# Last stage of a routed network: one sorted buffer of 136 tiles for two of 144, two routing batches, and a small GpSimd write ahead of each indirect transfer

## What is computed

```python
x = x + _L1_ffn_ref(_layernorm(x, axis=-1), router_w, w1, w2, w3)
...
h1 = jnp.einsum('nc,ehc->neh', flat, w1)
h3 = jnp.einsum('nc,ehc->neh', flat, w3)
h = jax.nn.silu(h1) * h3
y = jnp.einsum('neh,ech->nec', h, w2)
out = jnp.einsum('ne,nec->nc', gates, y)
```

## Time and profile before

| what | us |
|---|---|
| median of 3 runs | 1226.98 (1225.48 to 1228.63) |
| the profiled execution, by the clock of the runs | 1228.42 |
| its span in the profile | 1226.7 |
| mean clock granted to TensorE, as a share of 2.4 GHz | 0.952 |
| last stage: from its first up matmul to the end of the span | 809.3 to 1226.7 |
| last product (L1945) of the last stage starts | 1200.5 |

### The profile page before, as it was taken

One profiled execution on the slowest core, in us unless ns is written; L12 is line 12 of the kernel. 1 busy time (PEld: TensorE's weight loads), 2 busy tenths in 40 slices (PEclk: granted clock), 3 DMA queues, 4 the chain that ended last, 5 costly groups with the idle time before them and its releaser, 6 DMA issues.

```text
span 1226.7 us, 17966 instructions
## 1 busy us (share of the span) xinstructions
PE 1048.8 (85%) x5576; PEld 737.6 (60%) x5577; DVE 587.0 (48%) x1719; ACT 524.9 (43%) x980; POOL 502.7 (41%) x799
## 2 busy tenths in 40 slices
PE   4779966889998899998998989987779988988991
PEld 2334322567666544644873455467779888888891
DVE  7855873211064265555746634353273333333454
ACT  5567844234232476653357645544222222222220
POOL 5922265630633320000310366525336666565651
PEclk9799988999999999999999989999799999999996
DMA  9930001232322100000000111163255757668766
GB/s 278 365 154 1 1 33 63 78 93 69 94 78 78 29 18 0 1 1 0 1 1 1 64 43 45 38 179 112 78 180 187 242 167 258 189 225 312 239 199 226
DMA packets 100884, 135.53 MB, mean 110 GB/s; under 512 B 12434, under 2 KB 69570, under 8 KB 99906
## 3 DMA queue, kind: packets, MB, share of 16 engines
q1 hardware_dynamic: 88002, 108.00, 27.6%
q0 software_dynamic: 12800, 26.50, 6.6%
HBM read 88.81 MB, written 45.65 MB: 110 GB/s over the span
## 4 chain that ended last, share of the span: by engine, by line
PE 63%; DVE 14%; issue 8%; another core or an unknown queue 7%; ACT 5%; POOL 2%; DMA 1%; DVEq 0%; ACTq 0%; POOLq 0%; SPq 0%
PE bank L1263 14%; PE bank L1289 12%; PE bank L1270 9%; PE bank L1299 7%; PE bank L1148 4%; PE bank L1028 4%; PE bank L1183 2%; DVE sb_R L1945 2%; PE bank L1211 2%; PE bank L1200 1%; PE bank L994 1%; PE bank L1172 1%; DVE sb_R L1430 1%; PE bank L1192 1%
## 5 line engine op out<-in xcount | busy, mean ns | idle before, releaser
L1263 PE MATMUL bank<-sb_R,sb_wih_sb 128*128 128x512 f32 (+2 forms) x504 | 202.9, 553 | 12.5 <-ACT sb_R L879 6.6
L1945 DVE TENSOR_TENSOR sb_R<-sb_R,bank 114x384 f32<-114x384 f32 x144 | 79.6, 553 | 230.8 <-PE bank L1299 138.2
L879 ACT ACTIVATE sb_R<-bank,sb_lb_sb 128x512 f32<-128x512 f32 (+2 forms) x252 | 151.0, 633 | 88.6 <-PE bank L1270 78.4
L650 POOL DMA_INDIRECT expert_out<-sb_R,sb_slot_row x144 | 140.8, 977 | 111.3 <-DVE sb_R L1903 36.3
L913 ACT ACTIVATE sb_R<-bank 114x384 f32<-114x384 f32 x144 | 69.4, 490 | 250.0 <-PE bank L1289 123.4
L1263 PEld LDWEIGHTS bank<-sb_R,sb_wih_sb 128*128 128x128 f32 x504 | 96.4, 193 | 111.7 <-issue 82.7
L1289 PE MATMUL bank<-sb_xt,sb_BIG 128*114 128x128 f32 x864 | 111.0, 280 | 19.6 <-DVE sb_R L1945 15.0
L1299 PE MATMUL bank<-sb_BIG,sb_R 114*128 x864 | 123.6, 279 | 2.1 <-issue 1.6
L1289 PEld LDWEIGHTS bank<-sb_xt,sb_BIG 128*114 128x114 f32 x864 | 102.2, 183 | 23.9 <-issue 23.0
L644 POOL DMA_INDIRECT sb_R<-sorted_out,sb_dest_i x64 | 60.8, 950 | 125.7 <-DMA sorted_out<-sb_R 44.0
L1299 PEld LDWEIGHTS bank<-sb_BIG,sb_R 114*128 114x128 f32 x864 | 110.0, 194 | 2.5 <-issue 2.3
(11 more groups left out here) (279 smaller groups left out, 1691.5 us busy)
## 6 DMA issues: line engine op xcount, KB each, us to landing
sb_BIG<-up_t SPq DMA_DIRECT2D x72, 342.0 KB
sb_wih_sb<-up_t SPq DMA_DIRECT2D x36, 342.0 KB
sb_whh_sb<-up_t SPq DMA_DIRECT2D x36, 342.0 KB
sb_XS<-expert_in SPq DMA_DIRECT2D x18, 528.0 KB
expert_in<-sb_R SPq DMA_DIRECT2D x18, 512.0 KB, 6.0
sb_R<-expert_out SPq DMA_DIRECT2D x7, 1024.0 KB, 6.7
sorted_in<-sb_R SPq DMA_DIRECT2D x9, 512.0 KB, 5.5
sb_XS<-sorted_in SPq DMA_DIRECT2D x18, 256.0 KB
```

What stands on the lines that cost most here:

```text
L650: pool.indirect_dma_start(out=expert_out, out_offset=bass.IndirectOffsetOnAxis(ap=slot_row[:, i:i + 1], axis=0), in_=yd[i // 8 % RING][:, ...
L879: act.activation(gb[s][k][:, 0:c], bank[4 * s + k][:, 0:c], funcs[k], bias=lb_sb[:, (p - 1) * GATES + k:(p - 1) * GATES + k + 1]).then_inc ...
L1263: mm = pe.matmul(bank[4 * s + k][:, 0:c].rearrange("p (w b) -> p w b", b=GH), wih_sb[:, p - 1, k * P:(k + 1) * P], xin, start=True, stop=( ...
L1945: dve.tensor_tensor(hm[j % 2][0:HC, :], sl[j % 2][0:HC, :], bank[3 + 2 * (j % 2)][0:HC, 0:KU * P], ALU.mult).then_inc(d2_m, 1)
```

## The change

- The last stage has one sorted buffer, `expert_in`, of 136 tiles: 128 closed ones (`CLOSED1`) and one open tile for each expert, at the end. The tokens are placed in three batches (`BATCHES`): the first half of 32 token tiles as before during the LSTM, then two batches of 16. A batch fills whole tiles in the closed part; what is left over goes to the open tile of the expert, and a later batch fills that first.
- The loop has 17 groups of 8 tiles. Groups 0 to 6 need the first batch alone, groups 7 to 9 the second batch, and from the open group (10th in order) on they need the third (`READY` = 7, 10; `GROUPS`).
- The loop's extra work is put at other tiles: transposes and sums of the second half at tiles 0, 1, 2, 4, 6, 7, 8, 10, statistics in two batches, scores at 12 to 15 and 22 to 26, and each of the two batches is routed in 15 steps, one per tile, from tile 16 and from tile 30. The steps have more operations than before (`OpenPlaces`: 73 and 66 waiting operations for 47), on half as many tokens each. Two of the eight normalisations move from ACT to DVE.
- POOL's order is now 24 rows home, with the statistics ahead of rows 2 and 7, 32 sorting transfers (not before tile 28), 5 rows home, 32 sorting transfers (not before tile 52), 107 rows home (from tile 72), at the same pace of eight per five tiles. There are 392 indirect transfers.
- `pause()` stands ahead of every indirect transfer of the kernel, in the first expert layer too: POOL writes 0 to one column (`pause_p`, 128 x 1) and waits for the semaphore of that write.
- The loads of the final results start at group 14 of 17 (`D3_LOAD`), and their sums are spread over tiles 120 to 134.

```diff
+    CLOSED1 = 2 * NTILE
+    NS = CLOSED1 + E
+    BATCHES = ((0, NH), (NH, NH + NH // 2), (NH + NH // 2, NTILE))
+    READY = ((2 * NH - E + 1) // 8, (3 * NH - 2 * (E - 1)) // 8)
+    GROUPS = list(range(READY[1])) + [CLOSED1 // 8] + list(range(READY[1], CLOSED1 // 8))
...
-        T_TILES, RANK_TILE = 18, 21
-        Y_FIRST, IN_TILE, Y_TILE = 22, 26, 66
...
-        ND2 = HALVES * NSLOT1 // 8
-        D3_LOAD = ND2 - 5
+        T_AT = {1: 1, 2: 2, 4: 3, 6: 4, 7: 5, 8: 6, 10: 7}
+        XN_ACT_AT = {9: 0, 11: 2, 17: 4, 19: 5, 21: 6, 23: 7}
+        XN_DVE_AT = {9: 1, 11: 3}
+        R_AT = {12: 0, 13: 1, 14: 2, 15: 3, 22: 4, 24: 5, 25: 6, 26: 7}
+        ROUTE_AT = {1: 16, 2: 30}
+        HOME_FIRST, LN_AT, IN_AT, HOME_MORE, HOME_REST = 24, (2, 7), (28, 52), 29, 72
...
+        ND2 = NS // 8
+        HALF_GROUPS = (READY[1] + 1, ND2)
+        D3_LOAD = ND2 - 3
+        D3_ADD = 8 * (ND2 - 2)
...
             for g in range(1, ND2):
-                if g + 1 < ND2 and g + 1 != D2H:
+                if g + 1 < ND2 and g + 1 not in READY:
                     d2_load(g + 1)
+                if g == READY[0]:
+                    sp.wait_ge(rd.tiles, 2)
+                elif g == READY[1]:
+                    sp.wait_ge(rd.tiles, 3)
                 d2_weights(g)
-                if g + 1 == D2H:
-                    sp.wait_ge(s_scat[1][1], 32 * NH)
+                if g + 1 in READY:
+                    sp.wait_ge(s_scat[1][1 + READY.index(g + 1)], 16 * NH)
                     d2_load(g + 1)
...
+            def pause():
+                step(pool.memset(pause_p[:, :], 0.0))
+
...
                     for k in range(K):
+                        pause()
                         pool.indirect_dma_start(
...
             def rows_home(i):
+                pause()
                 pool.wait_ge(d2_yo, i + 1)
                 pool.indirect_dma_start(
...
+            def rows_in(b):
+                pool.wait_ge(rd.dest, b + 1)
+                lo, hi = BATCHES[b]
+                for i in range(2 * (hi - lo)):
+                    t, k = lo + i // 2, i % 2
+                    pause()
+                    pool.wait_ge(d2_h, IN_AT[b - 1] + 5 * i // 8)
+                    pool.indirect_dma_start(
+                        out=expert_in, out_offset=bass.IndirectOffsetOnAxis(ap=dest_i[:, k, t:t + 1], axis=0),
+                        in_=XR[:, t - NH, :], in_offset=None).then_inc(s_scat[1][b], 16)
...
+            for i in range(HOME_FIRST):
+                if i in LN_AT:
+                    t_finish(1, LN_AT.index(i), NGH // 2)
                 rows_home(i)
...
+            rows_in(1)
+            for i in range(HOME_FIRST, HOME_MORE):
+                rows_home(i)
+            rows_in(2)
+            for i in range(HOME_MORE, 8 * ND2):
+                pool.wait_ge(d2_h, min(HOME_REST + 5 * (i - HOME_MORE) // 8, 8 * ND2))
                 rows_home(i)
```

More of the change, by code:

```diff
@@ L444, in _ @@
             sp.wait_ge(w_in, W_ALL)
-            for rows in [sorted_in] + expert_in:
+            for rows in (sorted_in, expert_in):
                 zv = rows.rearrange("(p n) d -> p (n d)", p=P)
@@ L487, in d2_load @@
             def d2_load(g):
[L488 removed]
+                u = g % 2
                 if g >= 2:
@@ L616, in scatter @@
                     pool.wait_ge(zeroed, ZEROS)
-                rows, src = (sorted_in, XN[:, half * NH:(half + 1) * NH, :]) if layer == 0 else (expert_in[half], XR)
+                rows, src = (sorted_in, XN[:, half * NH:(half + 1) * NH, :]) if layer == 0 else (expert_in, XR)
                 for t in range(half * NH, (half + 1) * NH):
@@ L1029, in hidden, with rank @@
                               start=True, stop=True).then_inc(r.h, 1)
[L1031 to L1036 removed]
+            def rank(layer, r, b):
+                m = flat(space[layer, b].mask)
+                n = m.shape[1]
+                pe.wait_ge(r.mask, b + 1)
+                pe.matmul(bank[1][:, 0:n], before[:, :], m, start=True, stop=True)
+                pe.matmul(bank[1][:, n:2 * n], ones[:, :], m, start=True, stop=True).then_inc(r.ranks, 1)
             def b1_transposes(b):
@@ L1880, in _ @@
                         in_d[0].chosen(1)
-                    if half > 0 and n in (8, 9):
-                        in_d[0].weights(n - 8)
+                    if half > 0 and n == 8:
+                        in_d[0].weights(0)
+                    if half > 0 and n == 9:
+                        in_d[0].weights(1)
+                        in_d[0].weights(2)
                     if half > 0 and n == 10:
-                        in_d[0].counts()
+                        for part in range(3):
+                            in_d[0].counts(part)
                     if half > 0 and n == 11:
@@ L1922, in d2_slots, with d3_add, d2_route @@
                     dve.tensor_tensor(slot_row[:, cols], slot_k[:, cols], pad_row[:, cols], ALU.max).then_inc(d2_meta, 1)
-            def d3_add(i):
+            def d3_add(i, k):
                 t0, n = D3_BLOCKS[i]
                 xv = X[:, t0:t0 + n, :]
-                dve.wait_ge(y_in[i], 16)
-                for k in range(2):
-                    if k > 0:
-                        dve.wait_ge(d3_x, 2 * i + 1)
-                    dve.tensor_tensor(xv, both[i][:, :, k, :], xv, ALU.add).then_inc(d3_x, 1)
+                if k == 0:
+                    dve.wait_ge(y_in[i], 16)
+                else:
+                    dve.wait_ge(d3_x, 2 * i + 1)
+                dve.tensor_tensor(xv, both[i][:, :, k, :], xv, ALU.add).then_inc(d3_x, 1)
+            def d2_route(p, step):
+                if step == 0:
+                    p.scores()
+                    p.keys(0)
+                elif step == 1:
+                    p.chosen(0)
+                    p.second()
+                elif step == 2:
+                    p.keys(1)
+                elif step == 3:
+                    p.chosen(1)
+                elif step in (4, 5, 6):
+                    p.weights(step - 4)
+                elif step in (7, 8, 9):
+                    p.counts(step - 7)
+                elif step == 10:
+                    p.places()
+                elif step in (11, 12):
+                    p.rows(step - 11)
+                elif step == 13:
+                    p.table()
+                elif step == 14 and p.b == 1:
+                    p.carries()
             for part in range(3):
@@ L1982, in _ @@
             for i in D3_OF[1]:
-                d3_add(i)
+                for k in range(2):
+                    d3_add(i, k)
 def layouts(i):
```

459 lines of the change are left out of this document (261 added, 198 removed).

## The result

The changed kernel takes 1209.1 us in the median of its runs against 1226.2 us before, a ratio of 0.986 [0.982, 0.990]. The forecast was 1176: right in sign and inside its range, but the gain is 17 us where 50 were expected. The profiled run took 1216.6 us (span 1214.9), 7.5 above the median.

What follows compares the result with a forecast made beforehand. PE was taken to bound the kernel, its increments late while POOL issues indirect transfers back to back. 1228.4 less 43 us in the last stage and 8 in the rest gave 1177, or 1176 for a median; range 1150 to 1214.

Steps and rivals of the forecast that it cites:

- What bounds the kernel: Whole kernel: PE bounds it, 63% of the chain, its increments late while POOL issues indirect transfers back to back.
- the long stretch: Last stage, 98 tiles in 247.1 us before the change: 0.39 us too much per tile, 38 us to gain.
- Gain, if it separates the transfers so that increments come on time.: Write ahead of each transfer, last stage: gains 38 us in 98 tiles, 15.8 us at 851.8, 5.1 us at 909.8.
- The first rival: The write doesn't part the transfers, increments stay late: last stage 373 us, 23 less, 1210 in all; chance 0.20.
- The lone transfer: Last stage before the change: behind 1.46 us of POOL idling, silu starts 30 ns after its matmuls end.
- Price of a transfer with the write: POOL's cost per indirect transfer including the write: 1.31 us low end, 1.63 us high end, 1.50 taken.
- the third rival: POOL becomes the bound for good: break-even 1.75 us per transfer; at 1.9 us, 1269 us in all; chance 0.14.
- Tile 28 at 85 us: Last stage: without the 15.8 us stall at 851.8, tile 28 comes at 85 us instead of 100.6.
- POOL as the bound of the last stage: POOL's transfers end the last stage at 352.5 us, PE's own way at 324; before 396, so 43 us less.
- Routing and eight tiles: Last stage: two routing batches on DVE cost 6 us on PE's path; 8 fewer tiles save 17 to 20 us.
- SP's queue: Last stage: loads wait for 88 rows home, at 280 us, tile 115; group 15's weights wanted at tile 120; no cost.
- The rest of the kernel: Ahead of the last stage: lateness costs 13.5, 6.3 and 4 us, writes up to 15 us; net 8 us less.

Runs made afterwards that it cites:

- the two kinds of chip: On one, PE's increments come late beside POOL's transfers, unchanged kernel 1222.2 or 1226.2 us; on the other they don't, 1137.6 us.
- five writes: Changed kernel with five chained writes instead of one ahead of each last-stage transfer: 1308.6 us without late increments, 1340.7 us (one run) with them.
- the first pair: First timing of the unchanged and changed kernels, chip not known, increments late: 1226.2 us before, 1209.1 us changed, ratio 0.986.
- chip B: Second follow-up chip, increments not late: changed kernel 1138.1 us against 1137.6 before, ratio 1.001.
- chip C: Third follow-up chip, increments late, two sets of runs: unchanged kernel 1222.2 and 1222.5 us; changed 1213.0; without writes 1212.4 and 1214.3.
- the first kind: Chips on which PE's increments are not late: unchanged kernel 1137.6 us, changed 1138.1, changed without writes 1127.5.
- the run of twelve transfers: Twelve rows home in a row, in the changed kernel with the ninth row home held until the 21st tile's up product: 1227.6 us, increments late.

## Why the prediction was right and wrong

**What bounds the kernel.** Right for the chip it was read from: late increments beside POOL's transfers cost the kernel before 1226 - 1137 = 89 us, as the two kinds of chip show. The 38 us in the long stretch were the right size too: 2.52 against 2.16 us per tile, 35 us for 98 tiles. Too small was the share ahead of the last stage: the stage begins at 776 instead of 809 us in the kernel before, 33 us, where the forecast had 24 at most. Not seen, and not to be seen in one trace: that this is a trait of some chips, and that the other kind has none of it.

**"Gain, if it separates the transfers so that increments come on time."** This is the step that failed, worth the missing 33 us. A write with its wait lengthens the gap from 0.30 to 0.39 us, more than half of the increments stay late, and tiles in the long stretch are no shorter (2.59 us, before 2.52). The first rival described what happened: 373 us for the stage, 1210 us in all; measured 1192.21 + 0.96 - 815.2 = 378 us and 1209.1. "The gaps of 0.30 us don't help now, and 0.5 us may not either" deserved more than 0.20. The lone transfer of the earlier trace rows stood behind 1.46 us of idling, and no row showed anything between that and 0.30; in the gap of 1.34 us that five writes make, all increments on record are on time. Gaps between 0.39 and 1.34 us were not run, so where the change lies stays open.

**Price of a transfer with the write.** 1.50 taken; 1.35 measured, near the low end of 1.31. I had let the write wait behind the transfer's full gap, and it starts at once: 1055.67 is the end of the transfer at 1054.71. The next transfer starts 0.28 us after the write ends. From the rule of the Trainium skill (GPSIMD Engine Reference, "Instruction dispatch"), by which an instruction signals only when all eight cores are done, I had drawn the high end of 1.63 us and a parting of the transfers; the trace shows neither.

**The trade itself.** The working had both prices but not their product: to part 176 transfers by over 1 us asks for 2.3 us each, and the break-even of the third rival was 1.75. So the pause that is known to help makes POOL the bound: 1308.6 and 1340.7 us. Two or three writes, whose price would lie near the break-even, were not tried.

**Tile 28 at 85 us.** Measured 88, but luck has a part in it: the forecast had the stall go because the transfers are parted. Rows home start at 825 instead of 849.47, 10 us into the stage instead of 40, so eleven are never due together; holding them gives the stall back with the writes in place (101 us), and the old order keeps it with writes (99 us). The gain was booked under the write and belongs for the most part to the order.

**POOL as the bound of the last stage.** Wrong for the first pair: the last matmul ends at 1190.66, the last transfer starts at 1192.21. PE and POOL there:

```profile
1189.02 1.64 PE L1343 MATMUL bank<-sb_BIG,sb_R 114*128 x6 [0.31 <-DVE sb_R L2033]
```

```profile
1192.21 0.96 POOL L682 DMA_INDIRECT expert_out<-sb_R,sb_slot_row  x1 [0.28 <-issue]
```

Without lateness it is right in kind. End of the last stage of the changed kernel on chip B:

```profile
1118.84 0.96 POOL L682 DMA_INDIRECT expert_out<-sb_R,sb_slot_row  x1 [0.28 <-POOL sb_pause_p L640]
```

```profile
1112.90 0.35 DVE L2033 TENSOR_SCALAR sb_R<-bank,sb_slot_gate 128x128 f32<-128x128 f32 x1 [1.12 <-PE bank L1343]
```

POOL is 6 us behind, and its stage takes 1119.8 - 784.1 = 336 us. PE's own way, forecast as 324, is 323.8 us in the trace without writes.

**Routing and eight tiles.** Where nothing is late, from the ninth product to the 48th it takes 113.5 us without the writes against 102.3 before, 11 us more for the second batch and the new order; but the first eight tiles, from which work was moved, take 4.6 us less. Together 7 us, 6 forecast. The eight tiles fewer are worth 8 x 2.15 = 17 us.

**SP's queue: "Nothing."** Wrong where tiles take 2.1 us. SP and PE in the changed kernel on chip B:

```profile
1056.70 2.17 SPq L537 DMA_DIRECT2D sb_R<-expert_out  x4
1058.98 0.41 SPq L512 DMA_DIRECT2D sb_XS<-expert_in  x1
1060.13 9.17 SPq L524 DMA_DIRECT2D sb_BIG<-up_t  x4
```

```profile
1067.77 0.83 PE L1343 MATMUL bank<-sb_BIG,sb_R 114*128 x6
1074.93 2.45 PE L1333 MATMUL bank<-sb_xt,sb_BIG 128*114 128x128 f32 x10 [6.33 <-issue]
```

The forecast put the release of the loads at 280 us, tile 115; they are issued at 1056.7 - 784.1 = 273, tile 115. But they are four transfers of 1 MB ahead of the weights of group 15, and tile 120 waits 6.3 us. I had counted the queue's waits and not its bytes.

**The rest of the kernel.** Forecast 8 us less; the first product's matmuls start 6 us later than before (815.2, 809.2), but the eight traces of chip C have that start between 798 and 817, so nothing can be read from that. Without lateness it is 776.2 in both traces without writes and 778.1 to 784.1 in the six with them: the writes cost there, on average 4 us, and the first 64 sorting transfers take 91 us instead of 87; so they were on the path, as the forecast had it, though 4 us is less than its 15.

So the sum on the two kinds, by the traces, for the start of the last product. Late (the first pair): 20 us for eight tiles at 2.50 and 13 for the earlier 28th product, less 14 behind it (284.5 us for 108 tiles, which would take 270.4 at 2.50) and 6 ahead of the stage, is 13; the two products are 12.5 apart, the spans 11.8. Not late, without the writes: 17.2 for the tiles, 4.8 behind the 48th tile, most of it shorter waits for SP's weights (the kernel before has one of 7 us at tile 112, this one of 3.5 us at tile 120), and 4.6 for the first eight tiles, less 11.2 for the routing, is 15.4; so far apart are the products, the spans are 13 apart and the medians 10. The writes take these 10 us back.

## What to carry to other kernels

A cure is a claim with a dose: before a pause is put between two things, look in the trace for the shortest gap that is seen to help, multiply it by the number of times, and compare that with the slack of the engine that pays. When a stall goes, ask which part of the change removed it, the obvious one or the reordering beside it; one run that puts the old order back tells. And before tuning against a delay that the profile calls remote, run the unchanged kernel on another chip: here one per cent was won where the delay existed, and none where it didn't. Of the versions tried that give the reference's output, the one without any write is the one to keep: 0.990 of before where nothing is late, 0.990 and 0.992 where increments are, 11 us under the changed kernel on the first kind, level with it by the medians on the second.

## What the hardware showed that was not expected

One unchanged kernel takes 7 to 8% more on some chips than on others: 1137 us on two chips, 1222 us on a third, 1226 us for the first pair. Chip C was late in both of its sets of runs, ten minutes apart; whether it is the chip or a state that it was in, three chips can't tell. Durations are alike (the transfer home 972 and 977 ns, the product 554 and 553 ns in the kernel before); what differs is when PE's increments arrive beside GpSimd's indirect transfers. As far as the record goes it is PE's alone: ACT's and DVE's are on time in the same places. In the run of twelve transfers they come about 1 us after its end. POOL at work is not what holds them (with five writes it works between the transfers, and none on record is late), and the rows' traffic isn't either. Whether it is the spacing of the transfers or their rate that helps, and why some chips do this, was not found. The late kind also spreads more, 1197.7 to 1227.0 us over twelve runs of one kernel against 1136.0 to 1143.0, so a half per cent can't be told there with a dozen runs.
